# Zero rows fill the stacks of split queries and keys of the first layer's attention

## The reference

```python
D_MODEL = 128; N_HEADS = 16; HEAD_DIM = 8
qkv = x @ w_qkv + b_qkv
q, k, v = ...                                 # [B, H, T, 8], T = 512
att = jnp.einsum('bhqd,bhkd->bhqk', q, k) / jnp.sqrt(jnp.float32(Dh))
att = jnp.where(causal[None, None], att, -jnp.inf)
att = jax.nn.softmax(att, axis=-1)
y = jnp.einsum('bhqk,bhkd->bhqd', att, v)
return y.transpose(0, 2, 1, 3).reshape(B, T, C) @ w_proj + b_proj
```

## Time and profile before

| | us |
|---|---|
| median of 3 runs | 3398.66 |
| lowest and highest | 3397.5 and 3406.68 |
| span of the profiled execution | 3389.5 |
| TensorE matmul busy | 2579.8 (76%) |
| TensorE weight load busy | 1819.6 (54%) |
| VectorE busy | 1865.9 (55%) |
| ScalarE busy | 1591.1 (47%) |

### The profile page before, as it was taken

The page is one execution under the profiler, slowest core; times in us unless marked ns, Lnnn a source line. Parts: engine busy times, 40 slices in busy tenths (PEclk is TensorE's granted clock), DMA queues, the critical chain, the costliest instruction groups (busy, mean ns, idle before and its releaser), DMA issues. The chain is left out here.

```text
span 3389.5 us, 65593 instructions
## 1 busy us (share of the span) xinstructions
PE 2579.8 (76%) x23476; PEld 1819.6 (54%) x23508; DVE 1865.9 (55%) x4776; ACT 1591.1 (47%) x3545; POOL 932.4 (28%) x641
## 2 busy tenths in 40 slices
PE   2486888778788787878879678786888868787787
PEld 1254764456644565446645367453664447644565
DVE  2337654576445664466643765537655476545664
ACT  0137453474435643365434754338443474435644
POOL 1105330143303432043220442105330143302332
PEclk8588887888878888788878888789887888878888
DMA  3300011010110101001020010200002000110101
GB/s 96 84 5 10 14 26 73 4 15 12 38 60 1 16 15 59 35 3 16 13 89 5 5 18 9 89 5 10 13 19 80 4 13 13 33 64 4 16 15 42
DMA packets 213726, 96.60 MB, mean 29 GB/s; under 512 B 175978, under 2 KB 204530, under 8 KB 209754
## 3 DMA queue, kind: packets, MB, share of 16 engines
q1 hardware_dynamic: 209160, 90.02, 10.0%
q10 hardware_dynamic: 4224, 2.10, 0.2%
HBM read 70.88 MB, written 21.17 MB: 27 GB/s over the span
## 5 line engine op out<-in xcount | busy, mean ns | idle before, releaser
L1695 POOL TENSOR_TENSOR arena<-upto,gk 128x1536 f32<-128x1536 f32 x32 | 88.1, 2754 | 941.2 <-DVE beta L1142 941.2
L1149 DVE SCALAR_TENSOR_TENSOR arena<-bank,conv,arena 128x510 f32<-128x510 f32 (+1 forms) x384 | 285.7, 748 | 71.4 <-ACT arena L1442 47.8
L1687 POOL TENSOR_TENSOR arena<-arena 128x511 f32<-128x511 f32 x192 | 243.9, 1270 | 205.1 <-DVE arena L1149 204.9
L1036 DVE TENSOR_REDUCE mx<-bank 128x1 f32<-128x128 f32 (+3 forms) x512 | 219.0, 486 | 136.2 <-PE bank L515 131.2
L678 PE MATMUL bank<-h_t,arena 128*128 128x512 f32 x384 | 228.3, 690 | 57.1 <-DVE arena L1149 57.0
L514 PE MATMUL bank<-vq 72*128 72x128 bf16 (+3 forms) x512 | 180.9, 414 | 98.3 <-DMA vq<-qk_bounce 49.7
L1405 ACT ACTIVATE arena<-bank 128x384 f32<-128x384 f32 (+1 forms) x384 | 174.1, 538 | 166.2 <-PE bank L542 166.2
L1527 ACT COPY u<-bank 32x192 f32<-32x192 f32 x128 | 39.9, 312 | 400.2 <-PE bank L812 398.7
L1739 POOL TENSOR_TENSOR arena<-arena 128x1536 f32<-128x1536 f32 x24 | 82.5, 3437 | 422.7 <-DVE arena L1278 227.3
L469 PE MATMUL bank<-ident,xn 128*128 128x128 f32 x132 | 36.8, 435 | 169.5 <-DVE xn L987 169.5
L735 PE MATMUL bank<-vq 64*128 64x128 f32 x1536 | 117.2, 305 | 57.5 <-ACT arena L1516 36.5
(11 more groups left out here) (290 smaller groups left out, 6435.6 us busy)
## 6 DMA issues: line engine op xcount, KB each, us to landing
arena<-w_bounce SPq DMA_DIRECT2D x16, 1024.0 KB, 8.5
vq<-qk_bounce SPq DMA_DIRECT2D x27, 384.0 KB
vq<-qk_bounce SPq DMA_DIRECT2D x9, 1152.0 KB
qk_bounce<-qkp SPq DMA_DIRECT2D x54, 128.0 KB, 2.3
arena<-in_L_attn_Wv_dram SPq DMA_DIRECT2D x8, 768.0 KB, 11.7
t<-t_bounce SPq DMA_DIRECT2D x256, 12.0 KB, 1.8
x<-t_bounce SPq DMA_DIRECT2D x256, 12.0 KB, 1.8
arena<-in_L_attn_Wq_dram SPq DMA_DIRECT2D x8, 384.0 KB, 8.7
```

The costliest lines, as they stand in the source:

```text
L1036: last = V.reduce_max(mx[:, h, t:t + 1], score_bank(n)[:, 0:(t + 1) * P], AX.X)
L1149: ins = V.scalar_tensor_tensor(a[:, k:T], ps[:, 0:T - k], conv[:, n, 3 - k:4 - k], a[:, k:T], ALU.mult, ALU.add)
L1687: G.tensor_tensor(acc[:, n % 4, 1:T], acc[:, n % 4, 1:T], acc2[:, n % 3, 0:T - 1], ALU.add).then_inc(taps_added, 1)
```

## The change

The stacks are used over all 128 rows. Rows 0 to 71 are as before, rows 72 to 124 are zero in both stacks, and the rows of the maxima (in `k_stack` the ones) are the last three, 125 to 127 (`MS = 125`). `scores` now multiplies rows 0 to 124 and `scores_t` all 128, in as many matmuls, of as many columns, as before. The zeros come by DMA as well: VectorE makes 48 rows of zeros ahead of the loop, SP stores them as `zero_rows`, and in `enter_parts` SP loads 5 and 48 rows of them into each stack, ahead of the loads of the parts.

```diff
+    MS = P - PARTS
...
+        zero_rows = dram("zero_rows", [48, HA * T], BF16)
...
-                        mm(ps[:, 0:e], q_stack[0:KS, h, t * P:e], k_stack[0:KS, h, 0:e], start=True, stop=False)
+                        mm(ps[:, 0:e], q_stack[0:MS, h, t * P:e], k_stack[0:MS, h, 0:e], start=True, stop=False)
...
-                            mm(ps[:, c0:c0 + n], k_stack[0:KS + PARTS, h, j * P:(j + 1) * P], q_stack[0:KS + PARTS, h, j * P:T],
+                            mm(ps[:, c0:c0 + n], k_stack[:, h, j * P:(j + 1) * P], q_stack[:, h, j * P:T],
                                start=True, stop=False)
...
             V.memset(u32[:, :, :], 0.0).then_inc(xin_free, 1)
+            dve.wait_ge(rows_out, 16)
+            V.memset(q_stack[0:48, :, :], 0.0)
             V.memset(k_stack[0:PARTS, :, :], 1.0).then_inc(prologue_sb, 1)
...
             sp.dma_start(one_rows, k_stack[0:PARTS, :, :].rearrange("p h t -> p (h t)")).then_inc(out_sent, 16)
+            sp.dma_start(zero_rows, q_stack[0:48, :, :].rearrange("p h t -> p (h t)")).then_inc(rows_out, 16)
...
-            sp.wait_ge(rows_out, 16)
+            sp.wait_ge(rows_out, 32)
...
-                sp.dma_start(k_stack[KS:KS + PARTS, :, :].rearrange("p h t -> p (h t)"), one_rows).then_inc(stacks_in, 16)
+                sp.dma_start(k_stack[MS:P, :, :].rearrange("p h t -> p (h t)"), one_rows).then_inc(stacks_in, 16)
+                for stack in (q_stack, k_stack):
+                    for a, z in ((KS, KS + 5), (KS + 5, MS)):
+                        sp.dma_start(stack[a:z, :, :].rearrange("p h t -> p (h t)"), zero_rows[0:z - a, :]).then_inc(stacks_in, 16)
...
-                    sp.dma_start(q_stack[KS:KS + PARTS, HG * g:HG * (g + 1), :], m_bounce[g].rearrange("p (h t) -> p h t", t=T)).then_inc(m_in[g], 16)
+                    sp.dma_start(q_stack[MS:P, HG * g:HG * (g + 1), :], m_bounce[g].rearrange("p (h t) -> p h t", t=T)).then_inc(m_in[g], 16)
```

More of the change, by code:

```diff
@@ L21 @@
     "ln_var": 4, "ln_rstd": 4, "ln_xn": 4, "ln_ps": 4, "h_ready": 4, "dve_step": 221, "act_step": 21, "pool_step": 0,
-    "qk_ps": 2, "qk_f": 2, "qk_parts": 6, "rest_made": 4, "v_ps": 1, "v_ready": 1, "parts_out_q": 48, "parts_out_k": 48, "stacks_in": 80, "s_ps": 64,
+    "qk_ps": 2, "qk_f": 2, "qk_parts": 6, "rest_made": 4, "v_ps": 1, "v_ready": 1, "parts_out_q": 48, "parts_out_k": 48, "stacks_in": 144, "s_ps": 64,
     "s_max": 64, "m_parts": 4, "m_ps": 4, "m_sb": 4, "m_out": 64, "m_in_0": 16, "m_in_1": 16, "m_in_2": 16, "m_in_3": 16, "st_ps": 48,
```

## The result

| | before | after |
|---|---|---|
| median, us | 3402.67 (4 runs, 3397.5 to 3407.49) | 3458.6 (4 runs, 3454.47 to 3461.19) |
| ratio to before | | 1.0167, 95% interval 1.0141 to 1.0193 |
| span of the profiled execution, us | 3389.5 | 3459.5 |
| mean granted clock in it | 0.834 | 0.843 |

What follows compares the result with a forecast made beforehand. TensorE at half clock was taken to bound the attention's dense stretch. Costs of 5.9 + 4.9 + 3.5 + 2.0 us less 36 us gave -19.7 us, from 3398.7 to 3379 us, range 3364 to 3417.

Steps and rivals of the forecast that it cites:

- the price of the loads of zeros: Stack loads at each batch's start: zeros queued ahead of the parts delay the landing by 4.9 us.
- the lower end: Loads of zeros: 48-row loads spread over sixteen engines, 5-row loads over five; the landing moves by 4.9 us.
- My upper end: Loads of zeros: all 106 rows share three engines at 81 GB/s, 21.5 us.
- the stacks come late: Rival: 48-row loads don't spread, each turn's start waits for them; +126 us, 3524 us; chance 0.04.
- The turns: Seven turn changes: stacks land later, mostly covered because VectorE starts at 535.71; 0.5 us each, +3.5 us.
- Batch 0: Start of the kernel: 5.9 us for fill and store ahead of the loop, plus 4.9 us of uncovered landing.
- The end: End of the kernel: the unused stack loads land 4.9 us later, at 3388.9; cost 0, up to 2 us.
- The burst: Zeros moving on all engines at the second layer's end: 0.25 us in a batch, +2 us.
- The clock: First layer's attention: full clock within the dense stretch, also speeding the first `weigh`; 4.5 us a batch, 36 us saved.
- rises early: Rival: the clock is up before the dense stretch in each batch and holds; 47 us saved, 3368 us; chance 0.16.
- The clock doesn't rise: Rival: zero rows may not count as work, or float32 caused the rise; no gain, 3415 us; chance 0.15.
- busyness alone: Rival: only how busy TensorE is sets its clock, not rows; 3415 us, sharing the no-rise chance of 0.15.

Runs made afterwards that it cites:

- e1: A separate kernel of 16 KB row loads, each waited for, varying partitions and sources; 48 rows to partitions 77 to 124 took 7.66 us, 128 rows 7.75.
- e3: The changed kernel, but SyncE waits for the stacks to land before issuing a batch's weight loads; 3420.57 us, 1.0061 of the kernel before.
- e2: The changed kernel with its loads of zeros kept, but matmuls reading 72 and 75 rows as before; 3517.08 us, 1.0347 of the kernel before.
- e4: The changed kernel, but GpSimd fills the zeros instead of loads, and SyncE's load order is new; 3341.26 us, 0.9824 of the kernel before.
- e6: GpSimd-filled zeros and new load order, but `scores` reads 72 rows as before, `scores_t` all 128; 3347.46 us, 0.9853 of the kernel before.
- e5: GpSimd-filled zeros and new load order, but matmuls read 72 and 75 rows, ones and maxima in rows 72 to 74; 3393.96 us, 0.9995 of before.

## Why the prediction was wrong, point by point

**The step that failed is the price of the loads of zeros.** I reckoned that sixteen engines take three rows each at the 0.6 us that a row takes an engine when three engines work, so that the landing moves by 4.9 us. They did spread over sixteen engines (the share of 1.03 from 521 to 532 us), so the lower end's premise was right, but a row did not take 0.6 us then: the price per row came from three engines at 81 GB/s, sixteen engines at that pace would move 432 GB/s, and the zeros moved at 143. The nearest row for the total rate, 384 GB/s, was one of loads to 128 partitions. Neither showed 48 rows in 48 partitions by sixteen engines, and e1 does: 13.5 us for the two, set by the partitions that they go to. The landing moved by 12.0 us instead of 4.9. My upper end of 21.5 us covered this value, though for another reason; my choice between the ends did not, and the range left it out.

**The rival "the stacks come late"** had the right place and the right lever (each us at seven turns) and was given 0.04. Its chance was tied to one cause, few engines, when any cause of a late landing does the same; with 3 us between gain and none, the rival should have had a chance set by how little I knew of the term. What it missed is that the late landing runs into the weight loads: 5.3 us more at each turn (e3). The sign that I had named for it, a wait of TensorE for the stacks of more than 1 us at the turns, came true with 19.2 us; the other one, that the maxima's DMAs hold up `scores_t(0)`, did not: no wait of the change's first `scores_t` for them is in the trace.

**The turns.** Forecast +0.5 us each. Measured +17.3, less 3.4 in `scores`: 12.0 landing, 5.3 collision. The cover I named was right, VectorE is ready only at 557.1, 4.6 us after the last matmul of the batch, but it hides 4 to 5 us and no more.

**Batch 0.** Forecast 5.9 + 4.9 = 10.8 us, "scores some 11 us later"; measured 21.5. The fill was right (3.47 us, and 3.9 with its surroundings; forecast 3.7 and an issue), the store took 4.8 instead of 2.2 us (e1: a store of 48 rows takes as long as one of 128), and TensorE's wait for the stacks grew by 13.1 us (49.7 to 62.8) instead of 4.9. These add to 21.8 us.

**The end.** Forecast 0, up to 2 us; measured 8, because the unused loads of the last turn also land 12 us later.

**The burst** of the zeros at the second layer's end, forecast +2 us in all, can't be told apart: the rest of a batch is 2.1 us shorter in the change, but 1.3 us longer in e2, with the same loads and 75 rows, so a cost of up to about 1 us in a batch isn't excluded. Why the rest is shorter in the change stays open. The higher clock in the attention doesn't explain it, since e4 has that too and its rest is 341.2 us.

**The clock was right in size, and half right in its course.** Forecast -4.5 us in a batch, 36 in all; measured -3.3 in the dense stretch and -1.7 in the first `weigh`, 40 in all. The last rise came where I had put it, 2.4 to 5.4 us after the first `scores_t` in seven of eight batches. What I had not forecast is that the clock is also up for 6.8 to 10.2 us in `scores` and falls again as the dense stretch begins: this is the "rises early" of the rival, without its "holds". e6 shows my mechanism by itself, with 72 rows in `scores`: the rise comes 2.8 to 6.0 us into the dense stretch, and the stretch takes 8.0 instead of 10.7 us, 2.7 less (forecast 2.9). "The clock doesn't rise" is refuted, and so is busyness alone as the rule: TensorE is busy for 10.82 of 11.20 us in e2 and for all 11.20 us in e5 and stays at 0.50, and the same matmuls over 128 rows, 53 rows of them zeros, come up. The Trainium skill ("TensorE: Matmul & The Clock Gate", the part on the HAM clock gate) speaks of how busy the PE is and not of rows; this case's trace differs, and the trace decides. The medians of e5 and e4 differ by 53 us, more than the 40 of these stages; the profiled executions, 3395.3 and 3355.0 us in span, differ by 40.

**The chances.** 0.67 on faster rested on a clock term that held and on a cost term whose uncertainty was larger than the whole net gain of 20 us. Had the landing's 4.9 us stood as anything from 4.9 to 21.5, most of that span would have been slower.

## What to carry to other kernels

Filling the contraction rows of dense bf16 matmuls (the rows that a product is summed over) from 72 or 75 to 128 with zeros can raise TensorE's clock, which here was worth 53 us or 1.6% of the time, as long as the zeros cost nothing: write them by an idle engine, not by DMA. Price a load by the partitions it goes to and not by its bytes alone, and if a buffer arrives just in time, give every further us of landing the weight of the loop's length. Where a load repeats its source few times, look at the DMA share: it was 0.19 with a source repeated three times, and three loads of the keys took 9.5 us instead of 17.5.

## What the hardware showed that I had not expected

- A load of 48 rows of 16 KB to partitions 77 to 124 takes as long as one of 128 rows (7.66 and 7.75 us), a store likewise (6.25 and 6.27); to partitions 40 to 87 it takes 5.64, to every other one 5.49.
- 96 rows to partitions 0 to 95 took 8.66 us, longer than 128 rows to all. No run here explains it.
- Rows of zeros raise the clock: 0.50 for the whole dense stretch with 72 and 75 rows (e5), 0.77 on the mean of it with 125 and 128 (e4). Between e5 and e4 nothing else changed but the place of the rows of the maxima and the ones. How many rows are enough between 75 and 125, no run shows.
- Nine loads of 8 neighbouring rows for the queries and three of 24 for the keys instead of four loads gained next to nothing (31.9 to 29.6 us for all parts, when the keys alone go from 17.5 to 9.5). No run here explains it.
